# Dilated attention's query and key pieces: eight heads in one run of memory per dimension, stored in twelve transfers an image

## The reference, cut to what matters

```
qkv = x @ w_qkv + b_qkv        # q, k, v: (16, 16 heads, 784, 8)
for seg_len, r in zip([256, 512, 1024, 2048], [1, 2, 4, 8]):
    so = dilated_attention(q, k, v of the segment, in Hilbert order, r)
    out[segment] = so
return out @ w_out + b_out
```

## Time and profile before

| what | us |
|---|---|
| median of three runs (3945.85 to 3951.25) | 3948.46 |
| the profiled execution's own time | 3935.58 |
| its span, first to last instruction | 3933.8 |
| projection stage of the dilated layer (first store of pieces to last) | 2387.2 to 2527.3 |
| dilated attention (first load to last use of the tiles) | 2542.4 to 3215.8 |
| PE, DVE, ACT, POOL busy in the span | 3090.8, 2254.6, 1628.9, 858.4 |
| mean granted TensorE clock | 0.871 of full speed |

### The profile page before, as it was taken

The page is one execution under the profiler, slowest core; times in us unless marked ns, Lnnn a source line. Parts: engine busy times, 40 slices in busy tenths (PEclk is TensorE's granted clock), DMA queues, the critical chain, the costliest instruction groups (busy, mean ns, idle before and its releaser), DMA issues. The chain is left out here.

```text
span 3933.8 us, 73810 instructions
## 1 busy us (share of the span) xinstructions
PE 3090.8 (79%) x21356; PEld 1654.9 (42%) x21357; DVE 2254.6 (57%) x4064; ACT 1628.9 (41%) x3144; POOL 858.4 (22%) x1187
## 2 busy tenths in 40 slices
PE   6768699999999999775999318677878777535998
PEld 3335323333333333363666216444545545422336
DVE  6765487767777777164333225565555546554772
ACT  1105446666666666552111003444444444322440
POOL 0003201010010100163000571223222226770000
PEclk8989879999999999876999659879999986667996
DMA  2003612222122221111111113322232212111113
GB/s 70 0 6 146 174 33 49 44 44 44 36 49 44 44 42 26 57 39 38 42 41 41 39 37 103 110 60 52 43 58 47 47 37 82 45 43 51 53 53 111
DMA packets 209872, 214.45 MB, mean 55 GB/s; under 512 B 34083, under 2 KB 185828, under 8 KB 209636
## 3 DMA queue, kind: packets, MB, share of 16 engines
q1 hardware_dynamic: 195300, 185.43, 19.7%
q0 software_dynamic: 14336, 25.72, 2.2%
HBM read 128.48 MB, written 81.10 MB: 53 GB/s over the span
## 5 line engine op out<-in xcount | busy, mean ns | idle before, releaser
L998 ACT ACTIVATE attn_exps<-attn_sbank 128x392 f32<-128x392 f32 x1600 | 700.9, 505 | 435.5 <-PE attn_sbank L921 432.3
L1035 DVE TENSOR_REDUCE attn_mx<-attn_rot 128x1 f32<-128x784 f32 x768 | 709.8, 968 | 272.8 <-PE attn_rot L934 268.2
L921 PE MATMUL attn_sbank<-attn_q,attn_k 99*128 99x392 bf16 x1536 | 449.1, 336 | 33.8 <-issue 20.8
L934 PE MATMUL attn_rot<-attn_k,attn_q 96*128 96x392 bf16 x1536 | 405.2, 347 | 41.0 <-DMA attn_k<-k_pieces 19.4
L1623 ACT ACTIVATE dil_exps<-dil_sbank 128x512 f32<-128x512 f32 x512 | 288.6, 602 | 341.0 <-PE dil_sbank L1529 338.8
L1667 DVE TENSOR_REDUCE dil_mx<-dil_rot 128x4 f32<-128x1024 f32 x256 | 305.5, 1220 | 196.1 <-PE dil_rot L1539 195.8
L961 PE MATMUL attn_acc<-attn_exps,attn_v 128*32 128x392 f32 x3584 | 356.3, 510 | 0.0
L921 PEld LDWEIGHTS attn_sbank<-attn_q,attn_k 99*128 99x128 bf16 x1536 | 148.4, 97 | 308.3 <-ACT attn_exps L998 166.6
L2485 PE MATMUL silu_ph<-silu_route_w,silu_xT 128*128 x424 | 237.6, 645 | 18.0 <-issue 10.8
L1539 PE MATMUL dil_rot<-dil_k,dil_q 96*128 96x256 bf16 x1024 | 169.3, 292 | 86.3 <-DMA dil_k<-dil_k_pieces 50.2
L1883 POOL DMA_INDIRECT silu_rows<-r_xt,r_posi x224 | 217.8, 972 | 67.6 <-issue 67.3
(11 more groups left out here) (337 smaller groups left out, 5054.1 us busy)
## 6 DMA issues: line engine op xcount, KB each, us to landing
attn_q<-q_pieces SPq DMA_DIRECT2D x192, 98.0 KB, 3.3
attn_k<-k_pieces SPq DMA_DIRECT2D x192, 98.0 KB, 4.2
silu_x<-silu_rows SPq DMA_DIRECT2D x212, 64.0 KB, 1.7
dil_q<-dil_q_pieces SPq DMA_DIRECT2D x192, 66.0 KB
dil_k<-dil_k_pieces SPq DMA_DIRECT2D x192, 66.0 KB
q_pieces<-qkv_piece SPq DMA_DIRECT2D x16, 588.0 KB, 3.1
k_pieces<-qkv_piece SPq DMA_DIRECT2D x16, 588.0 KB, 3.2
silu_route_w<-L_w_in SPq DMA_DIRECT2D x32, 256.0 KB, 5.3
```

What stands on the lines that cost most here:

```text
L921: ins = nc.tensor.matmul(into[:, 0:HS], k_[t.side][g][:, j, c * P:(c + 1) * P], q[t.side][g][:, j, cols], start=True, stop=True)
L934: ins = nc.tensor.matmul(rot[b][:, hf, 0:HS], q[nxt.side][g][0:QROWS, j, c * P:(c + 1) * P], k_[nxt.side][g][0:QROWS, j, cols], start=True ...
L998: nc.scalar.activation(e_[:, n % NP, :], sbank[(n + t.side) % 3][:, 0:HS], ACT.Exp, scale=A_DIM ** -0.5).then_inc(s_ex, 1)
L1035: nc.vector.tensor_reduce(into, rot[b][:, :, 0:HS], AX.XY, ALU.max).then_inc(s_free, 1)
```

## The change

The two tensors in memory get the layout (piece, group, dimension, image, head in the group, token). For one piece, group, dimension and image, the rows of eight heads lie behind one another, 8 x 528 tokens or 8448 bytes. A load reads such a run for each of eight dimensions where it read 64 rows of 1056 bytes. The store has to split channels into heads and dimensions, which takes one transfer for each piece and group: 6 for q and 6 for k of 66 KB each in place of one of 396 KB each. The count that `s_stored` waits for goes from 4 to 14 transfers an image.

```diff
@@ dilated_inputs
-        STORED = 16 * 4
+        STORED = 16 * 14
@@
                         for t, dst in enumerate((qd, kd)):
                             sp.wait_ge(s_p3, 4 * i + 4 + 2 * j + t + 1)
-                            sp.dma_start(dst[:, :, bass.ds(img, 1), :].rearrange("p c b s -> c p (b s)"),
-                                         piece[j][t][:, :, :]).then_inc(s_stored[j], 16)
+                            for g in two:
+                                for p in range(PIECES):
+                                    sp.dma_start(dst[p, g, :, bass.ds(img, 1), :, :].rearrange("d b h s -> (b h) d s"),
+                                                 piece[j][t][64 * g:64 * g + 64, p, :]).then_inc(s_stored[j], 16)
@@ dilated_attention, load
-                            s = src[p, 64 * g:64 * g + 64, bass.ds(img.e, 1), :].rearrange("(h d) b s -> d h (b s)", d=D_DIM)
+                            s = src[p, g, :, bass.ds(img.e, 1), :, :].rearrange("d b h s -> d (b h) s")
@@ dilated_layer
-    qd = nc.dram_tensor("dil_q_pieces", (PIECES, P, B, OWN), bf16, kind="Internal").ap()
-    kd = nc.dram_tensor("dil_k_pieces", (PIECES, P, B, OWN), bf16, kind="Internal").ap()
+    qd = nc.dram_tensor("dil_q_pieces", (PIECES, 2, D_DIM, B, 8, OWN), bf16, kind="Internal").ap()
+    kd = nc.dram_tensor("dil_k_pieces", (PIECES, 2, D_DIM, B, 8, OWN), bf16, kind="Internal").ap()
```

## The result

The changed kernel takes 3960.19 us against 3950.23 for the kernel before on the same chip (medians of 22 runs each): 1.0021 times as long, 95% interval 1.0011 to 1.0031. The prediction was 3919 us and faster; the change makes the kernel slower, and the time lies inside the range only because the range took in the rivals.

A forecast was written before the change was run, and what follows sets the result against it. Slow loads of 80 to 120 GB/s, making TensorE wait in the attention, were taken as the bound. Loads -28.9, start -5 and stores +4.3 gave -29.6 us, 3919 from the median 3948.46; own range 3904 to 3935, whole range to 3966.

The forecast's parts named there:

- Stores: Projection stage: twelve stores at 0.49 us, 7.0 us an image on SyncE, hidden under 9.37; only the end shows, +4.3 us.
- the prediction's own signs of being wrong: Profile: load stretches staying at 77 to 119 GB/s, L1125 over 0.6 us, or "issue" gaps growing beside shorter waits.
- slow stores: Rival, projection stage: above 0.69 us pitch SyncE sets the pace; at 0.745 us +18 us instead of +4.3; 20% in all.
- Loads: Attention's loads: at 130 GB/s a group arrives 9.0 us after first issue, shortening TensorE's 13 gaps by 28.9 us.
- a cost on the reading side: Attention's loads: rates of 77 to 119 GB/s blamed on memory addresses, not partitions, hence 130 GB/s with longer runs.
- loads as they are: Rival, attention's loads: writing into eight partitions limits them; gaps gain 0 to 12 us, about 3946 us; 25%.
- The upper bound: Load rate: eight dimensions use at most half the sixteen engines, so half the stores' 338 GB/s, 169.
- a rule of the Trainium skill: Loads into SBUF: eight neighbouring partitions reach two of 16 ports, estimated 54 GB/s a transfer; change would bring only its tail.
- Start: Start of the attention: faster loads ahead of the constants let VectorE begin sooner, -5 us (0 to -6).
- "Issue" idling: Attention, TensorE idling behind the loop's jump: 31.2 us in 11 pieces, left at zero, -3 to +6 us.
- the 13% rival: Attention's loads: longer runs clog the eight partitions or instruction transfers, 3988 us; 13%.
- slow stores with unchanged loads: Rival case, projection stage and attention together: SyncE sets the stores' pace and loads get no faster, 3962 us; 8%.

The follow-up runs named there:

- e6: Kernel before, its two stores of pieces an image cut into twelve by piece and group, old layout, both sides cut alike: 3948.45 us, 1.0010 times the kernel before.
- e8: The changed kernel measured once more in a later group of runs: 3955.35 us, 1.0034 times the kernel before.
- e1: Kernel before with only the change's loads (runs of 8448 bytes), the two old stores kept; values not the reference's: 3934.42 us, 0.9974 times the kernel before.
- e9: The change's memory layout, but weight columns turned to (group, dimension, head), so six stores of 128 partitions an image: 3934.36 us, 0.9965 times the kernel before.
- the first: First comparison of the changed kernel with the kernel before: 3960.19 against 3950.23 us, 1.0021.
- e4: Kernel before with each load's eight rows on partitions twelve apart instead of neighbouring ones: 3940.80 us, 0.9993 times the kernel before.
- e3: Against the kernel before: turned weight columns, two stores, loads of eight 8448-byte runs lying together in one 66 KB block: 3946.42 us, 1.0000.
- e5: Turned weight columns, a load's eight runs in one 66 KB block, its rows on partitions twelve apart: 3925.83 us, 0.9951 times the kernel before.
- after: The changed kernel, set against the kernel before: 3960.19 against 3950.23 us, 1.0021.

## Why the prediction was wrong

**Stores: the step that failed.** The prediction took the issue time from the earlier trace rows "by tile and direction", 0.377 + 0.11 = 0.49 us, and concluded that SyncE keeps up and TensorE's projection covers it. A store takes 0.616 us for q and 0.607 for k, and with the gaps between instructions the pitch is 0.78 us on average. That is one of the prediction's own signs of being wrong (over 0.6 us). SyncE does not keep up: an image takes it 10.8 us, not 7.0, and the stage runs at its pace. The prediction also held that only VectorE's buffer waits for the values' stores; ScalarE waits for the same count, 12 times and 35.4 us in all. The rival "slow stores" had the mechanism, the place and the threshold right (0.69 us; e6 at 0.65 loses 8 us, mostly its tail, the change at 0.78 loses 30), and its witness, L1451 with 635 ns and two sides cut differently, came nearest. It was put at 20%, and its pitch of 0.745 us still gave 10.0 us an image and +18 us, where 10.8 and +30 were measured. The term was +4.3 us and measured +30; that alone turns the sign.

**Loads: right in direction, wrong in size.** -28.9 us were forecast from a distance of 9.0 us; it fell from 11.8 to 10.9, the waits inside the turns from 40.2 to 28.4 us (32.3 in e8), and the comparisons give -10 (e1), -16 (e9 and e8) and -22 us (the first). The failed step is "I take that for a cost on the reading side and so 130 GB/s". It was drawn from 77 and 119 GB/s with the same partitions. But the 119 (2651:2656) belong to a load of group 0 and the 77 (2782:2790) to one of group 1, and e4, with the same addresses and spread partitions, shows no difference between the groups. The reading side does matter (e3 against e9), but little; what holds the rate at about 100 GB/s are eight engines that write into eight neighbouring partitions (e4, e5). The rival "loads as they are", at 25%, named this; its 0 to -12 us were a little too low. The upper bound, half of the stores' rate or 169 GB/s, was far above what the change reached, 98 and 110 GB/s; the stores go the other way, out of 128 partitions into memory.

The prediction weighed a rule of the Trainium skill here, "SBUF — State Buffer", section on the DMA port swizzle: few partitions reach few ports. Its direction is borne out by the spread partitions, 17.2 GB/s an engine against 10.5. Its figure is not: the estimate that the prediction worked out from the page's 435 GB/s was 54 GB/s for one transfer into eight neighbours, and with transfers served one at a time 110 GB/s were measured (2687:2692 of after); the eight packets that open a turn's loads, 8448 bytes each in 0.61 us, give 111. The measurement decides.

**Start: wrong.** -5 us were forecast and nothing came. The queue got the constants out earlier (11.8 us behind the first load in place of 14.05), and they landed when they always did, behind 1.62 MB at 98 GB/s in place of 94.

**"Issue" idling and clogging.** 31.2 us before and after (30.0 in e8, 32.4 in e1): no effect of the longer runs shows in it, and the 13% rival did not happen; from first issue to release a load became shorter, not longer.

**The sum.** With the middle of the measured terms it would have been -16 (start included) + 30 = +14 us; the change itself measures +8 and +13. That 3960 lies close to the 3962 which the prediction gave to slow stores with unchanged loads (8%) is partly luck: the stores cost 30 us where that case had 18, and the loads gave back about 16 where it had little. The profile of before also happened to be a short one, 12.9 us under its median, as the prediction said, and so the difference of the two profiled executions (25.2 us) overstates the loss.

## What to carry to other kernels

Before one transfer is split into many, add up the queue: the issue time of exactly that shape, plus 0.1 to 0.2 us between instructions, times the number in a loop, against the time of the loop. Where no row shows the shape, the row with the same kind of split (sides cut differently) came nearest here (635 ns for 616), and the one with the same tile was far off (377); 0.13 us more of pitch for each of 192 stores cost 22 us. And where a layout must change so that loads get long runs, look first whether the producer can deliver it for almost nothing, as by turning weight columns: that kept the loads' gain and dropped all but 2.3 us of the price (e9, 0.9965 where the change has 1.0021 to 1.0034).

## What the runs showed of the hardware that was not expected

- The time in which SyncE issues a transfer depends on how both sides are cut, not on bytes: eight rows of 8448 bytes 277 ns and the same bytes as 64 rows of 1056 bytes 278 ns into eight neighbouring partitions; 474 ns (q) and 545 (k) for 64 partitions to 64 rows; 557 ns for 128 partitions to 16 by 8 rows; 616 ns (q) and 607 (k) for 64 partitions to 8 by 8; 643 and 696 ns into eight partitions twelve apart.
- A load into eight partitions keeps eight of sixteen engines busy, and the next one begins when those packets end (DMA share 50 to 56% under a full queue, and about 0.6 us between the starts of two transfers whose packets take 0.61 us).
- An eight-fold longer run changed an engine's rate by -11 to +11%; a transfer's eight rows spread over the tile made it 1.6 to 2 times as fast.
- Into neighbouring partitions the second group of a turn's loads has slower packets than the first (0.735 against 0.595 us in after); into spread partitions it has not (0.446 against 0.451 in e5).
- Into neighbouring partitions, eight runs read at once from one block of 66 KB are slower than eight that lie 135 KB apart (1.0000 against 0.9965 in time); into spread partitions they are not (0.9951 against 0.9965, intervals that overlap). Whether the cap that is left with spread partitions (18.5 GB/s an engine) is memory or the engine was not tried, nor was a second queue that would take the issue time of spread loads off SyncE.
